# Top-64 attention by threshold search: three rounds of counting in place of four, from a first guess made of the keys' mean and deviation

## The reference, cut to what matters

```python
scores = jnp.einsum('bhqd,bhkd->bhqk', Q, K) / jnp.sqrt(jnp.asarray(d, Q.dtype))
topk_scores, topk_idx = jax.lax.top_k(scores, topk)          # topk = 64 of 256
probs = jax.nn.softmax(topk_scores, axis=-1)
sel = gather(V, topk_idx)
return jnp.einsum('bhqk,bhkd->bhqd', probs, sel)
x = x + jnp.tanh(g_xattn[0]) * attention(layernorm(x), ctx, ctx, ...)
x = x + jnp.tanh(g_ffn[0]) * fp8_ffn(layernorm(x), ...)
```

## Time and profile before

| what | value |
|---|---|
| three timed runs | 3587.52, 3587.77, 3595.72 us, median 3587.77 |
| the profiled execution, its own time | 3593.15 us |
| its span, first to last instruction | 3590.8 us |
| busy: PE, DVE, ACT, POOL | 72%, 73%, 70%, 26% of the span |
| mean granted TensorE clock | 0.634 |
| rounds of counting | 64 groups x 4 = 256 |
| a batch (8 rounds) in the middle | 106 us |

### The profile page before, as it was taken

One profiled execution on the slowest core, in us unless ns is written; L12 is line 12 of the kernel. 1 busy time (PEld: TensorE's weight loads), 2 busy tenths in 40 slices (PEclk: granted clock), 3 DMA queues, 4 the chain that ended last, 5 costly groups with the idle time before them and its releaser, 6 DMA issues.

```text
span 3590.8 us, 76998 instructions
## 1 busy us (share of the span) xinstructions
PE 2571.7 (72%) x20752; PEld 1580.1 (44%) x20752; DVE 2616.6 (73%) x10729; ACT 2514.9 (70%) x6310; POOL 935.1 (26%) x1172
## 2 busy tenths in 40 slices
PE   4677767777777777776777777777777677776763
PEld 2344444444444444444444444444444444444442
DVE  2577777777777777777777777777777777777773
ACT  1577677777677777776777777777778677777773
POOL 5122222222222232222232222222232232232112
PEclk8566666666666665665566666666666666666555
DMA  3223232222222222232223232122232123232111
GB/s 67 44 31 54 42 52 51 39 53 49 45 52 46 45 53 49 46 58 39 46 46 57 46 55 49 39 55 48 45 58 48 36 49 53 46 57 32 27 24 41
DMA packets 452000, 168.11 MB, mean 47 GB/s; under 512 B 245616, under 2 KB 451440, under 8 KB 451520
## 3 DMA queue, kind: packets, MB, share of 16 engines
q1 hardware_dynamic: 451136, 162.38, 25.8%
q0 software_dynamic: 384, 0.33, 0.1%
HBM read 102.57 MB, written 59.24 MB: 45 GB/s over the span
## 4 chain that ended last, share of the span: by engine, by line
PE 33%; DVE 31%; issue 17%; ACT 15%; DVEq 2%; POOL 1%; ACTq 0%; DMA 0%; SPq 0%; POOLq 0%
ACT sign L1029 8%; PE ps_t L758 7%; PE ps_a L710 5%; DVE following L1350 4%; PE ps_a L720 3%; DVE masked L1344 3%; PE ps_t L786 3%; PE ps_a L858 3%; PE ps_o L846 3%; PE ps_t L790 2%; ACT act_junk L1036 2%; DVE score_sb L1244 2%; DVE above L1286 2%; PE ps_a L722 2%; DVE x_half L1255 2%
## 5 line engine op out<-in xcount | busy, mean ns | idle before, releaser
L1029 ACT ACTIVATE sign<-ps_t 128x512 bf16<-128x512 f32 x2048 | 1065.5, 611 | 99.0 <-PE ps_t L758 94.4
L758 PE MATMUL ps_t<-qs,ks 104*128 104x256 bf16 x4096 | 898.9, 348 | 236.2 <-DVE qs L1268 234.6
L768 PE MATMUL ps_c<-ones_b,sign 128*128 128x1 bf16 x8192 | 547.9, 171 | 168.0 <-ACT sign L1029 138.3
L768 PEld LDWEIGHTS ps_c<-ones_b,sign 128*128 128x128 bf16 x8192 | 427.2, 107 | 523.9 <-ACT sign L1029 504.8
L1036 ACT ACTIVATE act_junk<-score_sb,X 128x256 int8<-128x256 f32 x1024 | 510.7, 509 | 76.8 <-DVE following L1339 76.7
L758 PEld LDWEIGHTS ps_t<-qs,ks 104*128 104x128 bf16 x4096 | 354.6, 112 | 407.8 <-DVE qs L1268 304.0
L1047 ACT ACTIVATE unfit<-score_sb,thr 128x256 bf16<-128x256 f32 x1024 | 442.4, 531 | 108.1 <-DVEq L1448 98.9
L1344 DVE SCALAR_TENSOR_TENSOR masked<-score_sb,X 128x256 f32<-128x256 f32 x1024 | 490.9, 520 | 24.7 <-issue 1.3
L747 PE MATMUL ps_c<-identb,x_half 128*8 128x128 bf16 x512 | 87.7, 266 | 500.0 <-DVE x_half L1328 297.4
L1244 DVE TENSOR_SCALAR_CACHE_REDUCE score_sb<-ps_s 128x256 f32<-128x256 f32 x1024 | 388.6, 417 | 55.1 <-PE ps_s L736 41.8
L1268 DVE COPY qs<-x_rows 8x2048 bf16<-8x2048 bf16 x256 | 194.7, 761 | 288.4 <-ACT x_rows L1024 285.1
(11 more groups left out here) (167 smaller groups left out, 4437.3 us busy)
## 6 DMA issues: line engine op xcount, KB each, us to landing
rows<-q_scr SPq DMA_DIRECT2D x192, 128.0 KB, 5.1
rows<-k_scr SPq DMA_DIRECT2D x192, 128.0 KB, 4.9
o_scr<-o_sb SPq DMA_DIRECT2D x128, 128.0 KB, 5.0
q_scr<-split SPq DMA_DIRECT2D x32, 384.0 KB, 2.7
k_scr<-split SPq DMA_DIRECT2D x32, 384.0 KB, 2.9
x_in<-in_x SPq DMA_DIRECT2D x32, 256.0 KB, 3.7
ctx_sb<-in_ctx SPq DMA_DIRECT2D x32, 256.0 KB, 3.7
v_scr<-proj SPq DMA_DIRECT2D x32, 256.0 KB, 3.0
```

The costliest lines, as they stand in the source:

```text
L758: ins = nc.tensor.matmul(ps_t[:, bank, kc * TOK:(kc + 1) * TOK], ks[u][0:M_ROWS, h, 8 * kc:8 * kc + 8, :].rearrange("d j t -> d (j t)"), q ...
L768: ins = nc.tensor.matmul(ps_cnt[par][:, 2 * n + jh:2 * n + jh + 1], sign[:, buf, kc * TOK + jh * P:kc * TOK + jh * P + P], ones_b[:], star ...
L1029: nc.scalar.activation(sign[:, buf, :], ps_t[:, bank, :], ACT.Sign).then_inc(s_G, 1)
```

## The change

`GUIDES` goes from 4 to 3. The first trial of a row is `q.mean + 0.6745 * deviation`, both from the keys of the head taken as independent dimensions. For that:

- POOL squares the key projection (a 128 x 512 multiply behind the splits); DVE sums keys and squares over tokens (`sum_keys`, two reductions of 128 x 512); PE brings the sums into 16 x 32 (`key_moments`, 2 small matmuls); ACT copies them (`evacuate_moments`); DVE turns them into weights (`weigh_keys`, 6 small instructions).
- In the last round of a group PE multiplies the queries with these weights (`gauss`, 16 matmuls of 17 columns), ACT squares and copies the result (`evacuate_gauss`), and `start_thresholds` reduces it, takes a root by bits, and forms the first trial.
- The Newton step is scaled by that deviation and no longer by the row's largest score.

What four rounds held is dealt out over three: the finals in chunks of 3, 3, 3, 3, 2, 2 tiles, scores and exponents in 3, 3, 2 heads (a third exponent inside a round, `MIX_LAG` 3, three mask buffers), mixing by pairs of heads. Jobs of other batches move with it, and on ACT the evacuations of projections stand behind the first mask of a round and ahead of its other masks and final counts. `f_sb` and `xq_sb` become one buffer, and some tiles share storage, with waits for it.

```diff
-GUIDES = 4
+GUIDES = 3
-START = 0.25
-SLOPE = 0.0040 / 2
+START = 0.6745
+SLOPE = 0.0115 / 2
+CHUNKS = ((0, 1, 2), (3, 4, 5), (6, 7, 8), (9, 10, 11), (12, 13), (14, 15))
+HEADS = ((0, 1, 2), (3, 4, 5), (6, 7))
-MIX_LAG = 2
-FINAL_SPLIT = (((0,), (1, 2, 3, 4)), ((5,), (6, 7, 8, 9)), ((10,), (11, 12, 13)), ((14, 15), ()))
+MIX_LAG = 3
+FINAL_SPLIT = (((0,), (1, 2, 3, 4, 5)), ((6,), (7, 8, 9, 10, 11)), ((12, 13), (14, 15)))
...
+            def gauss(i, b, u, g, bank):
+                pe.wait_ge(s_W, b + 1)
+                for n in range(GH):
...
+                        ins = nc.tensor.matmul(ps_t[:, bank, (D + 1) * t:(D + 1) * (t + 1)],
+                                               qs[u][0:D, h, 8 * jh:8 * jh + 8, :].rearrange("d j t -> d (j t)"),
+                                               gauss_w[:, h, :], start=True, stop=True)
+                ins.then_inc(s_gs, 1)
...
                         if mixes:
-                            masks_of(2 * mb + mg, 2 * mp + mg, 2 * r)
-                            masks_of(2 * mb + mg, 2 * mp + mg, 2 * r + 1)
-                        for t in FINAL_SPLIT[r][1]:
-                            final_counts(2 * b + g, 2 * p + g, t)
+                            masks_of(2 * mb + mg, 2 * mp + mg, HEADS[r][0])
...
                         if has(2) and (g, r) == (1, 0):
                             evacuate_projection(b + 2, 1)
-                        if has(2) and (g, r) == (1, 3):
+                        if has(2) and (g, r) == (1, 2):
                             evacuate_values(b + 2)
-
+                        if mixes:
+                            for n in HEADS[r][1:]:
+                                masks_of(2 * mb + mg, 2 * mp + mg, n)
+                        for t in FINAL_SPLIT[r][1]:
+                            final_counts(2 * b + g, 2 * p + g, t)
...
             def start_thresholds(i, slot):
-                dve.wait_ge(s_copied, GH * i + GH)
+                dve.wait_ge(s_ge, i + 1)
...
-                nc.vector.tensor_scalar(x_half[slot % 2][:], mx[:, slot, :], START, None, ALU.mult)
+                nc.vector.tensor_reduce(variance[:], gauss_sq, AX.X, ALU.add).then_inc(s_st, 1)
...
+                root(sd[:], variance[:]).then_inc(s_st, 1)
...
+                nc.vector.scalar_tensor_tensor(x_half[slot % 2][:], sd[:], START, gauss_mean[:],
+                                               ALU.mult, ALU.add).then_inc(s_st, 1)
...
                         ending = final_thresholds(i, slot) if last else iter(())
+                        if last:
+                            next(steps, None)
                         for _ in ending:
                             next(steps, None)
```

More of the change, by code:

```diff
@@ L795, in exponent_taken, with count_round @@
                 pe.wait_ge(s_PT, 16 * b + GH * g + n + 1)
-            def count_round(b, p, u, g, r, phase, first, second, middle):
+            def count_round(b, p, u, g, r, first, second, third, middle, starts):
                 i, slot = 2 * b + g, 2 * p + g
-                bank = [(phase + r + k) % BANKS for k in range(GH + 2)]
-                buf = [sign_buffer(phase, r, n) for n in range(GH)]
-                of_round = [k for k in range(GH + 2) if k not in (0, 5)]
+                buf = [sign_buffer(r, n) for n in range(GH)]
                 def difference(n):
-                    differences(i, u, g, r, n, bank[of_round[n]])
+                    differences(i, u, g, r, n, bank_of(r, OF_ROUND[n]))
                 def counted(n):
@@ L915, in batch, with middle @@
                     for r in range(GUIDES):
[L916 to L919, removed]
+                        first, second = lagged(HEADS[r][0]), lagged(HEADS[r][1])
+                        third = lagged(HEADS[r][2]) if r < GUIDES - 1 else None
+                        starts = (2 * (b + 1) + g, b + 1, (u + 1) % OPS, g) if r == GUIDES - 1 and has(1) else None
+                        def middle():
+                            if r < GUIDES - 1 and has(1):
+                                scores(b + 1, (u + 1) % OPS, g, HEADS[r][2])
+                            if r == 0 and mixes:
+                                sum_unsure(2 * mb + mg, 16 * (b + 1) + GH * g + 2 if has(1) else 16 * NB)
                         if r:
@@ L1533, in batch, with copies @@
                     guided = g == 0 or has(1)
+                    def copies(n):
+                        if has(1):
+                            copy_scores(i + 2, fresh, n, 0)
+                            copy_scores(i + 2, fresh, n, 1)
                     for r in range(GUIDES):
-                        finals = final_tiles(i, slot, r)
+                        last = r == GUIDES - 1
+                        free = FINAL * i + 1 + 2 * CHUNKS[2 * r + 1][0]
+                        finals = final_tiles(i, slot, 2 * r)
                         next(finals)
@@ L1538, in batch @@
                             place_thresholds(i + 1, cu, cg, r)
[L1539 to L1542 removed]
+                        next(finals)
+                        copies(HEADS[r][0])
+                        copies(HEADS[r][1])
+                        next(finals, None)
+                        if (g, r) == (0, 0):
+                            transpose_maxima(b)
@@ new lines, in batch @@
+                        if has(-3) and (g, r) == (1, 1):
+                            finish(b - 3, 1 - p, free)
+                        if has(-2) and (g, r) == (1, 2):
+                            update_residual(b - 2, p)
+                        if has(2) and (g, r) == (1, 2):
+                            sum_keys(b + 2)
+                        if r == 0 and mixes:
+                            settle(i - 1, mixed, free)
+                        finals = final_tiles(i, slot, 2 * r + 1)
+                        next(finals)
@@ L1566, in batch @@
+                        next(finals)
+                        if not last:
+                            copies(HEADS[r][2])
+                        next(finals, None)
                         if last and has(1):
```

338 lines of the change are left out of this document (226 added, 112 removed).

## The result

| | before | after |
|---|---|---|
| median of 4 runs | 3591.39 us (3587.52 to 3595.72) | 3881.4 us (3871.88 to 3888.16) |
| ratio, 95% interval | | 1.0805 (1.0777 to 1.0833) |
| span of the profiled execution | 3590.8 us | 3886.3 us |
| mean granted clock | 0.634 | 0.615 |

The account below looks back on a forecast made before the run. No engine by itself bounds the kernel; a loop of waits between engines does. Batches +64, ends -23 and missed tiles +41 make +82 us: 3670 us against a median of 3587.77, with 3465 to 3765 us for 8 in 10.

Parts of the forecast that it names:

- The wait for counts 14 and 15 in each last round: Last round of each group: counts stand behind the projection's evacuation and delay the update, 7.2 and 7.6 us of new wait.
- The walk of the six rounds: One batch, place to place: 13.9, 15.6, 21.5, 18.5, 13.7 and 25.1 us, 108.3 against 106.15 before.
- The rival of the full clock: Projections on PE run at 2.4 GHz, not half clock: 101.3 us a batch, 3460 us in all; chance 17%.
- POOL beside DVE: Group 1, round 2: new start falls at POOL's copy; charged nothing beyond 15.6, with 0 and 3 us per batch as ends.
- DVE falls behind POOL: Rival: 3 us of DVE stalls per batch on top, 111.3 us a batch, 3760 us in all; chance 15%.
- The rule that I weighed: DVE beside POOL: new reductions free of stalls; the root, the guess and the cast behind them not.
- Missed tiles, +41: Full selection: 9 tiles in 8 groups with rows missed by the search, against 5 tiles before; 93 us against 52.
- The ends, -23: Before the first batch -9 us, batch 30 -8 and batch 31 -6, together -23 us.
- Sum: Whole kernel: +64 - 23 + 41 = +82 us, 3670 us against the timed median, 2.3% slower.

Follow-up runs that it names:

- e1: Changed kernel with the final counts of tiles 14 and 15 ahead of the signs again in a group's last round: 3440.46 us, 0.9592 of the kernel before.
- e3: Changed kernel with POOL's two large copies moved, queries' between the splits, keys' behind the next layer norm: 3751.48 us, 1.0455 of the kernel before.
- e10: Kernel before, four rounds, with POOL's two large copies moved (queries' between the splits, keys' behind the next layer norm): 3559.34 us, 0.9922 of the kernel before.
- e4: Changed kernel with ACT's copies of projections and tokens behind all masks and final counts of their round: 3453.69 us, 0.9622 of the kernel before.

## Why the prediction was right in sign and wrong in size

- *The wait for counts 14 and 15 in each last round* (called decisive): right. From the read to the next place pass 14.7 and 15.3 us in the trace, where 12 to 14 and 15 to 16 were forecast, and of these DVE waits 7.29 and 9.67 us for the counts. e1 shows that the wait costs 441 us.
- *The walk of the six rounds*: right for four of them within 0.8 us, and for the other two but for POOL. (The terms of round 1 of group 1 add up to 13.5 and not 13.7.) Its rows for the projections held: PE worked without a gap at half clock through the value projection. The stretch 2215 to 2221 (length, busy PE, PEld, DVE, ACT, POOL, granted clock):

```profile
2215.00:2221.00 6.00, 6.00 (x12) 3.13 (x12) 0.00 (x0) 0.00 (x0) 1.49 (x4) 0.50 0.15 44
```

  The granted clock was 0.50 through the two projections on the path as well (2152.55 to 2156.33 and 2174.87 to 2178.63). The rival of the full clock is out, although a stretch in which PE idles shows more (0.83 from 2156.4 to 2166.6, PE busy for 2.52 of 10.20 us).
- *POOL beside DVE, "I cost it at nothing beyond 15.6"*: this is the step that failed. Both ends of its range (0 and 3 us per batch) were too low. The rows of before show the old start held for 2.08 us; I saw that the new start falls at the same copy of POOL and charged it nothing. In the changed kernel the root in it is held a whole copy long (3.61), so that the counts are read 12.5 us after the place and not 9.3. In the round ahead a masked tile (3.70) is held by the other copy, and the place (1.42) by the new squaring. Their excess is 3.43 + 3.2 + 0.7 = 7.3 us per batch. e3 took them away from there: the two rounds got 6.6 us shorter on average, 1.3 came back in round 0 of group 1, and 130 us were saved in all, 4.3 for each of 30 batches. The rival "DVE falls behind POOL" (15%) had the mechanism, with 3 us per batch where the excess is 7.3. The rest of the excess of 7.0 us is round 0 of group 0 (+0.8) and the last round of group 0 (+0.6; from 2159.39 to 2166.66 the end took 7.27 us in place of 5.85, with three of its steps held beside POOL's splits), less what the walk had too long in rounds 1 and 2 of group 1 (0.6 to 0.7 each).
- The rule that I weighed (the Trainium skill, SBUF — State Buffer, "Who interferes with whom") held in the rows shown here. It says that copies, casts and `tensor_scalar` can contend, which is weaker than "do" in the prediction. A reduction beside a multiply of POOL (2134.16, 1.26 us) took its 0.69, and the `tensor_scalar` behind it was still held:

```profile
2134.22 0.69 DVE L1645 TENSOR_REDUCE rowmax<-masked 128x2 f32<-128x512 f32 x1
2134.94 0.51 DVE L1647 TENSOR_SCALAR nanrow<-rowmax 128x2 f32<-128x2 f32 x1
```

  The root, a `tensor_scalar`, and the masked tile, with two SBUF inputs, were held. I had named the root as what is not free, and then charged nothing for it. That was my error and not a gap of the rule.
- *Missed tiles, +41*: the price was right (10.6), the count off by one tile (10, not 9): +53 us.
- *The ends, -23*: nearly right, though not in their parts. By the places of the two traces, the part ahead of batch 0 is 2.4 us shorter (9 forecast), batch 30 is 6.9 shorter (8 forecast), and all from batch 31 on is 0.8 longer, with one missed tile in it; without that tile, at 10.5 us, it is 9.7 shorter (6 forecast). Together -19 us.
- *Sum*: the profiled executions are 295.5 us apart (3590.8 and 3886.3), 213.5 more than the forecast's 82. Batches 0 to 29 are 304.0 us longer. Four more missed tiles stand in them (42 us by the forecast's price), so 262 us are the batches themselves (8.7 each) where 64 were forecast: 198 of the shortfall. The tiles are 12 and the ends 4. Of the 198, e3 shows POOL's two copies to be 139 (its profiled execution, 130 by the medians). Some 59 are left to the small terms above, and no run separates these.

## What to carry to other kernels

When a table deals work anew over fewer rounds, look at which of its entries another engine's last step waits for: two counts of 0.5 us behind a copy that waits for a projection cost 14.7 us per batch, and moving two numbers turned a loss of 8% into a gain of 4%. A hold by another engine's long copy is to be charged at up to the full length of the copy when the held instruction stands ahead of a read or a place, as in rounds 1 and 2 of group 1 here; where DVE had waited for ACT in the same round, 3.3 us of hold cost 1.0 (e3). Moving such a copy moves the hold, so look at what stands at its new place. Two cures of one wait don't add up, while a cure of another cause does. And before two runs are compared, compare the work that depends on the data: three more full selections hid half of what e10's edit gave.

## What the runs showed of the hardware that I had not expected

An instruction of 0.17 us on 128 x 16 elements is held by POOL's copy for all of its 3.6 us, not slowed in proportion: the root ends with the copy in the changed kernel and in e4 alike (3.61 and 3.62 us). The 16 `gauss` matmuls of 17 columns took 0.56 us together. With ACT's two evacuations behind them (1972.96 to 1973.45, 0.5 us) that is some 1.25 us from the first to the last, near the lower end of the 1.0 to 2.0 allowed for both:

```profile
1972.20 0.56 PE L797 MATMUL ps_t<-gauss_w,qs 16*128 16x17 bf16 x16
```
